# First maxima run beside a value product cut into four parts, one unit's split and writes moved back, one read moved forward

## The reference, cut to what matters

```
xq = (x @ wq + bq).reshape(B, S, 32, 16); xk, xv = the same with 8 heads
q, k = rope(xq), rope(xk)                       # two halves of 8, cos and sin by token
scores = einsum('bqhd,bkhd->bhqk', q, k) / 4    # each key head serves 4 query heads
probs = softmax(scores, axis=-1)
out = einsum('bhqk,bkhd->bqhd', probs, v)
```

## Time and profile before

| what | value |
|---|---|
| median of 3 runs | 1590.36 us (1590.22 to 1595.71) |
| profiled execution | 1585.47 us, its span 1583.6 us |
| PE busy | 1262.9 us, 80% of the span |
| DVE busy | 1004.4 us, 63% |
| POOL busy | 747.7 us, 47% |
| ACT busy | 627.4 us, 40% |
| chain that ended last, by engine | PE 19%, DVE 12%, POOL 4%, issue 4%, ACT 2%, DMA 1%, SPq 1% |

### The profile page before, as it was taken

How to read it: one execution, slowest core, us unless ns; L and a number is a source line. 1 busy time by engine, 2 the same in 40 slices (tenths; PEclk the granted TensorE clock), 3 DMA queues, 4 the chain that set the end, 5 groups by cost and what they waited for, 6 DMA issues and landing times. The chain is left out here.

```text
span 1583.6 us, 18591 instructions
## 1 busy us (share of the span) xinstructions
PE 1262.9 (80%) x6071; PEld 890.6 (56%) x6071; DVE 1004.4 (63%) x1724; ACT 627.4 (40%) x1174; POOL 747.7 (47%) x750
## 2 busy tenths in 40 slices
PE   2768999999999999999999999667959999951000
PEld 0447776776776777777777777556734334321000
DVE  4644655656655665655656565656558888537888
ACT  0323333333333434333333433235306777744223
POOL 2236756655756657656756756566210012041006
PEclk8789999999999999999999999879868998975555
DMA  5120122122222221121221120310574310000001
GB/s 179 54 64 20 59 69 71 59 72 67 60 74 67 60 74 42 58 74 46 59 69 55 53 67 20 102 59 1 111 123 60 48 55 2 2 1 0 0 0 53
DMA packets 71136, 87.53 MB, mean 55 GB/s; under 512 B 6921, under 2 KB 40873, under 8 KB 70466
## 3 DMA queue, kind: packets, MB, share of 16 engines
q1 hardware_dynamic: 69170, 83.63, 19.6%
q10 hardware_dynamic: 1872, 2.72, 0.5%
HBM read 78.54 MB, written 7.52 MB: 54 GB/s over the span
## 5 line engine op out<-in xcount | busy, mean ns | idle before, releaser
L1633 POOL TENSOR_TENSOR sw<-sw,sinT 128x512 f32<-128x512 f32 x80 | 103.1, 1289 | 142.6 <-ACT sw L1360 142.6
L1169 DVE TENSOR_REDUCE nm<-banks 128x2 f32<-128x1024 f32 x128 | 152.0, 1219 | 24.4 <-PE banks L738 23.6
L1409 ACT ACTIVATE yTh<-yF 128x512 fp32r<-128x512 f32 x64 | 40.4, 632 | 319.6 <-DVE yF L1026 319.6
L1645 POOL TENSOR_TENSOR dec<-gb,gcol 128x512 f32<-128x512 f32 x64 | 70.3, 1098 | 202.7 <-DVE Sd L992 194.8
L1515 ACT ACTIVATE Pb<-banks 128x512 f32<-128x512 f32 x256 | 134.9, 602 | 48.0 <-PE banks L759 47.6
L588 PE MATMUL banks<-st,qt 128*128 128x128 f32 x384 | 82.0, 298 | 52.8 <-DVE Sd L992 27.7
L536 PE MATMUL banks<-hTh,wgh 128*128 128x512 f32 x256 | 121.7, 475 | 0.0
L964 DVE SCALAR_TENSOR_TENSOR gs<-tg,banks 128x512 f32<-128x512 f32 x64 | 44.0, 687 | 119.5 <-ACT tg L1367 119.5
L536 PE MATMUL banks<-hTh,wqh 128*128 128x512 f32 x256 | 108.1, 422 | 0.0
L616 PE MATMUL banks<-woh,yTh 128*128 128x512 f32 x256 | 103.5, 404 | 2.1 <-DVE yTl L1029 2.1
L589 PE MATMUL banks<-xc,Sd 128*128 128x128 f32 x512 | 97.8, 290 | 5.0 <-DVE Sd L992 5.0
(11 more groups left out here) (305 smaller groups left out, 3412.3 us busy)
## 6 DMA issues: line engine op xcount, KB each, us to landing
gb<-g_scr SPq DMA_DIRECT2D x64, 256.0 KB, 3.5
raw<-in_wmod SPq DMA_DIRECT2D x40, 256.0 KB, 2.7
raw<-in_wo SPq DMA_DIRECT2D x32, 256.0 KB, 2.8
raw<-in_wq SPq DMA_DIRECT2D x31, 256.0 KB, 2.7
raw<-in_wg SPq DMA_DIRECT2D x31, 256.0 KB, 2.7
qsT<-q_scr SPq DMA_DIRECT2D x24, 256.0 KB, 7.8
q_scr<-hl SPq DMA_DIRECT2D x32, 128.0 KB, 3.3
mt<-mods_scr SPq DMA_DIRECT2D x12, 256.0 KB, 4.7
```

Of the source, the lines that this page charges most:

```text
L1169: ve.tensor_reduce(nm[:, b, i, p:32:16], pairs[z_][:, :].rearrange("p (g t) -> p g t", g=2), AX.X, ALU.max, negate=True).then_inc(*v_nm.up ...
L1633: po.tensor_tensor(s_[:, :], s_[:, :], sinT[:, :], ALU.mult).then_inc(*g_rope.up("sin", kind, t, n))
L1645: po.tensor_tensor(dec[:, :, :], gb[s % 2][:, :, :], bc(gcol[:, t % 2, heads(t), n], 2, 128), ALU.subtract).then_inc(*g_dec.up("sub", s))
```

## The change

The value product becomes four calls, `vproj(b, j)`: the waits in front stay with part 0, the semaphore and ACT's copy with part 3. The line of first maxima is made in `story` and handed to both functions. In `parts(1)`, each of the four parts is followed by three steps of the line; `attentions` takes the other four. `high`, `low` and `stow` of unit 1 of batch 1 leave `parts` and stand behind `scored(0, 0)`. In batch 0 the first placement of queries, `place_q(0, 0, 0)`, is issued right behind the writes of unit 0, ahead of the writes of unit 1; the other three follow as before, but for their order.

```diff
-        def vproj(self, b):
+        def vproj(self, b, j):
...
-            for j in range(4):
...
+            if j == 3:
+                mm.then_inc(*p_qkv.up("v", b))
+                self.drain[6] = a_qkv("v", b)
...
-    def parts(E, b):
+    def parts(E, b, line):
...
         E.proj(b, g1)
         E.high(b, g0), E.low(b, g0), E.stow(b, g0)
+        if b == 0:
+            E.place_q(b, g0, 0)
         E.prod_u(b, g1)
         E.comb(b, g1)
-        E.vproj(b)
-        E.high(b, g1), E.low(b, g1), E.stow(b, g1)
+        for j in range(4):
+            E.vproj(b, j)
+            if b:
+                line.step(), line.step(), line.step()
         if b == 0:
-            for m in range(2):
-                E.place_q(b, g0, m), E.place_q(b, g1, m)
+            E.high(b, g1), E.low(b, g1), E.stow(b, g1)
+            E.place_q(b, g1, 0), E.place_q(b, g0, 1), E.place_q(b, g1, 1)
...
-    def attentions(E, pending):
-        line = stream(E, pass_a_line)
-
+    def attentions(E, line, pending):
...
-        for _ in range(16):
+        for _ in range(4):
             line.step()
         scored(0, 0)
+        E.high(1, 1), E.low(1, 1), E.stow(1, 1)
...
-        parts(E, 0)
-        parts(E, 1)
+        line = stream(E, pass_a_line)
+        parts(E, 0, line)
+        parts(E, 1, line)
```

More of the change, by code:

```diff
@@ L703, in proj @@
                 self.drain[bk] = v_qkv(b, u, n if u == 2 else 2 + n)
-        def vproj(self, b):
+        def vproj(self, b, j):
             pe = self.e
[L707 to L711, removed]
-            for j in range(4):
[L713 to L721, removed]
+            if j == 0:
+                if b == 0:
+                    pe.wait_ge(*v_aw("v"))
+                    pe.wait_ge(*d_a[2]("rows"))
+                    pe.wait_ge(*g_vp("two"))
+                pe.wait_ge(*self.drain[6])
+            o, sl = banks[6][:, j * 128:(j + 1) * 128], slice(j * 128, (j + 1) * 128)
+            c = 0
+            for k in range(4):
+                for x_, w_ in ((hT2h, vwh), (hT2h, vwl), (hT2l, vwh)):
+                    pe.matmul(o, x_[b][:, k, sl], w_[:, k, :], start=(c == 0), stop=False)
+                    c += 1
+            mm = pe.matmul(o, one2[:, :], brow[:, :], start=False, stop=True)
+            if j == 3:
+                mm.then_inc(*p_qkv.up("v", b))
+                self.drain[6] = a_qkv("v", b)
         def pass_a(self, b, p, i):
@@ L1477, in bias, with vproj @@
                 ac.activation(bcol[:, :], banks[bk][:, 0:6], ACTF.Copy).then_inc(*a_fT.up("bias"))
-        def vproj(self, b):
+        def vproj(self, b, j):
+            if j < 3:
+                return
             ac = self.e
@@ L2421, in story @@
         middle(E)
-        parts(E, 0)
-        parts(E, 1)
+        line = stream(E, pass_a_line)
+        parts(E, 0, line)
+        parts(E, 1, line)
         pending = joined(stream(E, head, 0), stream(E, mixes, 0))
-        attentions(E, pending)
+        attentions(E, line, pending)
         pending.rest()
```

## The result

The changed kernel takes 1578.59 us (median of 4 runs, 1575.66 to 1579.99) against 1590.59 us (1590.22 to 1595.71). The ratio is 0.9926, 95% interval [0.9903, 0.9949]; two later comparisons gave 0.9935 [0.9908, 0.9963] and 0.9948 [0.9931, 0.9964]. So it is faster by 8 to 12 us. The forecast was 1579.9 us. The profiled execution has a span of 1573.8 us, against 1583.6 us.

A forecast was written before the change was run, and what follows sets the result against it. DVE's wait for a key write behind twelve reads was taken to bound the stretch. 11.25 us gained at the first score, less 0.7 for a bank, gave 10.5 us: 1579.9 us from the median 1590.36, range 1573 to 1587.

The forecast's parts named there:

- What bounded before: Before the first maxima: DVE idles 16.41 us for batch 1's low key write, which stands behind twelve query reads of 2.26 us.
- The reads: Ahead of the first pair: unit 1's third read lands at 1154.3 instead of 1157.0, bounds 1153 to 1160.
- The stretch of maxima: Maxima beside the value product, half clock from 1159.4: first score at 1179.0 instead of 1190.25, a gain of 11.25 us.
- a lower bound: Mixed stretch: if the clock already falls in front of value part 1, the gain is 1.4 us less.
- pair 6: Mixed stretch: the sixth pair of first-pass scores ends at 1162.0, having waited for maximum 4.
- The full-clock rival: Mixed stretch keeps 2.4 GHz and DVE alone bounds: first score about 1173, gain 17 less 0.7, 1574.0 us; chance 0.18.
- The bank for the second `max_part`: Behind the first score: bank 6 is free 5.4 us after it, transposes before ran at 4.76; PE loses 0.7 us.
- The small DMAs of group 1: Behind the first score: group 1's first score waits for its two DMAs, costing 1 to 2 us, 1581.5 us; chance 0.14.
- one of my signs: Trace after: PEclk is 0.5 from about 1159 until some 10 us behind the first score.
- one to one: From the first score to the end: a gain at that score is carried through attention and mixing block in full.
- Slower: Rival: PE waits before its first pair with value parts 1 to 3 behind it; read 16 us late, 1596 us; chance 0.05.
- late reads: Rival: unit 1's third read lands at 1158 to 1160, everything 3 to 5 us later, 1584 us; chance 0.15.

The follow-up runs named there:

- the dense mix: Changed kernel with the value product in sixteen pieces, one step of first maxima and two unread 512-column matmuls behind each; 1585.39 us.
- defer_only: Changed kernel with the value product whole again and all 16 steps of first maxima behind it, late split and early read kept; 1577.40 us.
- no_read_ahead: Changed kernel with all four placements of batch 0's queries behind the writes again; 1580.29 us.
- read_ahead_only: Kernel before with nothing but the early read of batch 0's queries; 1583.44 us, ratio 0.9965.
- parted_only: Changed kernel with batch 1's unit 1 split and writes back in front of the value product, parts and early read kept; 1594.22 us, ratio 1.0041.

## Why the prediction was right, point by point

**What bounded before** (the key write behind twelve reads): right, and shown to carry the gain. Taking `high`, `low` and `stow` out of that place, and nothing else, gives 0.9923 and 0.9948; putting them back, with all else kept, gives 1.0041. The early read alone (0.9965) works on the same wait and adds nothing that shows once the wait is gone.

**The reads.** I had the third read of unit 1 land at 1154.3, 27.95 us behind the mark. In the first profile it landed at 1149.0 (issued 1141.1, 7.9 us to landing), 27.5 behind the mark, and the first pair, which waited 0.70 us, came at 27.6. Right. The writes did nothing to batch 1's unit 0, as said.

**The stretch of maxima.** I had S0 at 1179.0, that is 52.65 us behind the mark; the three profiles have 52.6, 52.2 and 52.2. Behind V I had it at 25.8; the second and third profiles have 25.4. In the first the agreement is in part luck: V came 1.6 us earlier than in the rows, and V to S0 took 27.5 us, 1.6 us more than forecast, since the read held the first pair up and the clock fell as part 1 began instead of behind it, which I had as a lower bound (1151.8, 5.2 us behind V; I had 6.2). Half clock came in all three, a part took 3.15 us for 3.1, and the wait of 0.99 us in front of each third pair is of the kind that I worked out for pair 6 (0.5 us). The gain at S0 is 63.7-52.3 = 11.4 us for 11.25. The full-clock rival did not happen in any profile of the changed kernel. The Trainium skill's rule that an idle time throttles and activity releases (page "TensorE: Matmul & The Clock Gate", section "What's actually happening") is not borne out here if activity means the profile's busy share: in the dense mix TensorE was busy for 31.00 of 31.00 us and stayed at 1.2 GHz.

**What the parting is worth.** The prediction added the parts into the sum as if they were the way to the gain. It worked out S0 only for the whole change and never for the deferral alone; with its own rows that is 7.2 us for the value product, and 17.2 us from the earlier trace rows (1190.25-1173.05), hence 1153.16+7.2+0.9+17.2 = 1178.5, within 0.5 us of the 1179.0 for the whole change. That comparison was missing, not a wrong term. The first maximum comes 5.9 us earlier with the parting (29.0 against 34.9), but at half clock each part costs PE 3.15 us, for 0.60 to 2.60 us of which DVE waits, and M1 to S0 is 23.2 to 24.5 us instead of 17.2: 6.0 to 7.3 us come back.

**Behind the first score.** The bank for the second `max_part`: I had it free 5.4 us after S0 and a loss of 0.7; the transposes started 5.22 us after, with 0.39 us of waiting, a loss of 0.46. Right. The small DMAs of group 1 were issued 9.1 to 10.5 us after S0 and group 1's first score came after 16.9, with no idle time of PE in front of it, so that rival did not happen. What I had not priced, and one of my signs has wrong, is the clock's return: I had it some 10 us behind the first score, and it came 18.4 to 18.7 us behind it. Behind the mark it came at 70.6 to 71.3 us in the changed kernel and at 74.0 and 81.5 in the kernel before, so it did not move up by the 11.4 us that the first score did. The times show it: group 1 came after 16.9 us in all three profiles of the changed kernel, but after 14.0 and 16.4 in the two of the kernel before. At half clock one block of keys takes 4.07 us (1181 to 1185), at full 2.61. From S0 to the last product with the values it is 212.8 us against 206.5 and 212.3. So 0.5 to 6.3 us of the 11.4 are given back, and the gain at S0 was not carried to the end at one to one: it leaves 5 to 11 in single profiles and 8.3 to 11.8 by the ratios. In six profiles with the deferral (the changed kernel three times, the deferral alone twice, defer_only) this stretch is 212.3 to 212.8 us, and 206.4 in no_read_ahead; in the four without it (the kernel before twice, read_ahead_only, parted_only) it is 206.5, 212.3, 205.6 and 208.1. That leans to a real cost, but it is too few to show one; it stays open.

**The total.** The forecast of 1579.9 us lies 1.3 us from the measured median. The mechanism earns the 8 to 12 us; that the two agree this closely is luck, with executions of one kernel up to 19 us apart and three comparisons that give 8.3, 10.3 and 11.8 us for a forecast of 10.5.

**Slower and late reads.** Not here; but the slower rival's mechanism, a wait before a pair holding the value product back, is what the parting without the deferral showed at 1.0041; there the wait was for DVE's maximum in front of the third pair, not for a read in front of the first.

## What to carry to other kernels

When an in-order engine stands before a wait, look first for the instruction that waits and needs not be there yet; moving it behind the next stage's start may be all of the gain, and work woven into the gap may be worth nothing, or cost 8 us where the wait is still there. Work out each edit alone, the smallest one above all, from the same rows. Compare two profiles from a mark just before the change, or the clock of a stage 500 us away will be booked on it.

## What the hardware showed

TensorE at 100% busy in the profile is no sign of full clock: it stayed at 1.2 GHz for 31 us of unbroken work in one kernel and for 13 us of it (1200 to 1213) in the second profile of the kernel before. Executions of one kernel differ by up to 19 us (1580 to 1599), and where between 140 and 950 us the first short stretch of half clock comes (at 250, 490 or 610 us, or none) is one part of it that the traces show: the mark is at 1131.5 to 1137.0 us where it comes at 250, at 1126.1 to 1127.3 at 490 or 610, and at 1121.5 to 1124.9 with none.
